# Softmax attention on paired 64-row tiles: fp32r stacks, three score banks, values in two parts of 256 queries, outputs normalised on GpSimd

## The reference

```python
qkv = x @ qkv_w.T + qkv_b                       # x: [4, 1024, 256]
qkv = jnp.transpose(qkv.reshape(B, S, 3, 16, 16), (2, 0, 3, 1, 4))
q, k, v = (qkv[0], qkv[1], qkv[2])              # [4, 16 heads, 1024, 16]
scores = jnp.einsum('bhqd,bhkd->bhqk', q, k) / sqrt(16)
attn = jax.nn.softmax(scores, axis=-1)
out = jnp.einsum('bhqk,bhkd->bhqd', attn, v)
out = jnp.transpose(out, (0, 2, 1, 3)).reshape(B, S, E)
return out @ out_w.T + out_b
```

## Time and profile before

| | |
|---|---|
| median of 3 runs | 2549.8 us |
| profiled execution, own time | 2556.4 us |
| its span, first to last instruction | 2554.6 us |
| mean granted TensorE clock | 0.942 |
| busy: PE, DVE, ACT, GpSimd | 2278.0, 1613.1, 1345.3, 644.6 us |
| stages (us of the span) | projection 0 to 119.5, attention to 986.8, feed-forward to 1221, the rest to 2554.6 |
| maxima on DVE (L509) | 512 of 1220 ns |
| exponentials on ACT (L667) | 1024 of 598 ns |
| scores, maxima, values on PE (L574, L567, L582) | 1024, 1024, 2048 instructions |

### The profile page before, as it was taken

How to read it: one execution, slowest core, us unless ns; L and a number is a source line. 1 busy time by engine, 2 the same in 40 slices (tenths; PEclk the granted TensorE clock), 3 DMA queues, 4 the chain that set the end, 5 groups by cost and what they waited for, 6 DMA issues and landing times. The chain is left out here.

```text
span 2554.6 us, 41316 instructions
## 1 busy us (share of the span) xinstructions
PE 2278.0 (89%) x14644; PEld 1462.9 (57%) x14644; DVE 1613.1 (63%) x2762; ACT 1345.3 (53%) x2589; POOL 644.6 (25%) x407
## 2 busy tenths in 40 slices
PE   7779999999999994787579999999999999588886
PEld 4412222222222222676568888888888888477775
DVE  5588788877878852677435445454545534568876
ACT  5517777777777773454254344444434444354551
POOL 3400000000000000355423325233332523234432
PEclk9859999999999997898789999999999999799998
DMA  6831211211121002111330213121220311200100
GB/s 193 241 77 54 55 40 39 73 41 39 39 73 41 6 7 88 34 50 50 120 100 26 93 38 105 52 67 52 67 93 28 115 51 59 66 17 26 33 17 25
DMA packets 129296, 159.02 MB, mean 62 GB/s; under 512 B 29896, under 2 KB 111952, under 8 KB 125008
## 3 DMA queue, kind: packets, MB, share of 16 engines
q1 hardware_dynamic: 129104, 156.47, 20.6%
HBM read 117.76 MB, written 38.27 MB: 61 GB/s over the span
## 5 line engine op out<-in xcount | busy, mean ns | idle before, releaser
L509 DVE TENSOR_REDUCE att_sb_mx<-att_ps_psM 128x1 f32<-128x1024 f32 x512 | 608.4, 1220 | 151.0 <-PE att_ps_psM L567 143.7
L667 ACT ACTIVATE att_sb_pt<-att_ps_psS 128x512 f32<-128x512 f32 x1024 | 586.2, 598 | 209.4 <-PE att_ps_psS L574 193.7
L574 PE MATMUL att_ps_psS<-att_sb_q,att_sb_k 99*128 99x512 bf16 x1024 | 392.7, 386 | 30.5 <-ACT att_sb_pt L667 12.0
L574 PEld LDWEIGHTS att_ps_psS<-att_sb_q,att_sb_k 99*128 99x128 bf16 x1024 | 96.9, 96 | 458.4 <-ACT att_sb_pt L667 406.4
L567 PE MATMUL att_ps_psM<-att_sb_k,att_sb_q 96*128 96x512 bf16 x1024 | 321.2, 396 | 28.5 <-DVE att_sb_ident_b L503 23.2
L582 PE MATMUL att_ps_psO<-att_sb_pt,att_sb_v 128*32 128x512 f32 x2048 | 273.9, 607 | 1.0 <-ACT att_sb_pt L667 1.0
L163 POOL MEMSET ffn_sb_half<- 128x4 f32 x1 | 0.1, 107 | 853.5 <-POOLq L184 853.5
L1922 ACT ACTIVATE gla_sb_sg<-gla_ps_psP 128x512 f32<-128x512 f32 x64 | 38.2, 598 | 277.1 <-PE gla_ps_psP L1683 277.1
L2256 POOL TENSOR_TENSOR gla_sb_dm<-gla_sb_dm,gla_sb_masked 128x1024 f32<-128x1024 f32 x64 | 158.5, 2498 | 90.5 <-DMA gla_sb_dm<-decay_rows 90.2
L1939 ACT ACTIVATE gla_sb_dm<-gla_sb_dm,gla_sb_neg_g 128x128 f32<-128x128 f32 x512 | 156.4, 391 | 10.1 <-POOL gla_sb_dm L2256 10.1
L567 PEld LDWEIGHTS att_ps_psM<-att_sb_k,att_sb_q 96*128 96x128 bf16 x1024 | 99.1, 100 | 107.7 <-DVE att_sb_mx L509 31.3
(11 more groups left out here) (256 smaller groups left out, 4917.0 us busy)
## 6 DMA issues: line engine op xcount, KB each, us to landing
gla_sb_dm<-decay_rows SPq DMA_DIRECT2D x32, 1024.0 KB, 5.8
gla_sb_eg<-decay_exp SPq DMA_DIRECT2D x64, 256.0 KB, 6.7
qk_parts<-qkv_sb_part SPq DMA_DIRECT2D x64, 192.0 KB, 3.1
values<-qkv_sb_va SPq DMA_DIRECT2D x32, 256.0 KB, 3.5
att_sb_v<-values SPq DMA_DIRECT2D x32, 256.0 KB, 3.7
att_sb_q<-qk_parts SPq DMA_DIRECT2D x32, 192.0 KB, 3.1
att_sb_k<-qk_parts SPq DMA_DIRECT2D x32, 192.0 KB, 3.0
qkv_sb_xin<-in_x SPq DMA_DIRECT2D x8, 512.0 KB, 5.1
```

The costliest lines, as they stand in the source:

```text
L509: nc.vector.tensor_reduce(mx[:, t // NT, t % NT:t % NT + 1], psM[:, t % 2, :], AX.X, ALU.max).then_inc(maxima_free, 1)
L574: pe.matmul(psS[:, j % 2, :], k[0:ROWS, g, j, s * P:(s + 1) * P], q[0:ROWS, g, qh, j, :], start=True, stop=True).then_inc(scores_done, 1)
L667: nc.scalar.activation(pt[:, s % 2, j, :], psS[:, j % 2, :], ACT.Exp).then_inc(exp_done, 1)
```

## The change

- **Stacks.** Queries and keys are split into two fp32r parts instead of three bf16 ones. A stack has three blocks (`Q_PART`, `K_PART`), 48 rows, and 2 rows for the maximum, against minus ones on the keys' side. The heads of a pair stand two and two: even heads in SBUF rows 0 to 63, odd heads in rows 64 to 127. A score matmul uses one half of the rows, the maxima matmul written beside it the other.
- **Score banks.** `psS` has three banks instead of two; the bank for the outputs' transposes (`psX`) goes, and the maxima are turned in the ring itself, at step 5 instead of 2.
- **Values** go in two parts of 256 queries, behind the third and the fourth score of a step.
- **Maxima** run half a unit less ahead (`AHEAD = 8` tiles beyond the next unit), 24 tiles in the prologue. GpSimd splits them (two operations instead of DVE's four).
- **Outputs.** They are not transposed any more. Four DMAs lay the sums out on 128 partitions (`den`), DVE takes the reciprocal, it goes to DRAM and back as a broadcast (`rb`), GpSimd multiplies 128x512, and SP stores the outputs with features on rows (`att_t`). All in `sums` and `out` on SP and `normalize` on GpSimd.
- **SP's order** per unit is `sums` of the unit before, in first halves the load of a later pair, the maxima rows of the next unit (the fourth waits for GpSimd's multiply), the outputs' store.
- **Projection.** Weights and tokens are split into two fp32r parts and multiplied in three passes; ACT writes one part, DVE the other.
- **Feed-forward.** `turn_projected` and `copy_projected` go; two DMAs a tile load the attended tokens as they are needed.

The core of the diff:

```diff
-Q_PART = (0, 1, 2, 0, 0, 1)
-K_PART = (0, 1, 0, 1, 2, 0)
+Q_PART = (0, 0, 1)
+K_PART = (0, 1, 0)
 STACK = len(Q_PART) * AD
-ROWS = STACK + 3
+ROWS = STACK + 2
+HALF_PE = P // 2
...
+        PASSES = ((whi, xhi), (whi, xlo), (wlo, xhi))
...
-        psS = m.ps("psS", [P, 2, ST])
+        psS = m.ps("psS", [P, 3, ST])
         psO = m.ps("psO", [P, ST])
-        psX = m.ps("psX", [P, NT, P])
...
+            def rows(b, g, qh, finished=None):
+                u = unit(b, g, qh)
                 sp.wait_ge(rows_ready, u + 1)
+                for a in range(2):
+                    for r in range(2):
+                        p = HALF_PE * r + STACK + a
+                        if a and r and finished is not None:
+                            sp.wait_ge(on_ready, finished + 1)
+                        sp.dma_start(q[p:p + 1, g, qh, :, :].bitcast(F32).rearrange("p j t -> p (j t)"),
+                                     mrow[TILES * a + 8 * r:TILES * a + 8 * r + 8, :].bitcast(F32)).then_inc(rows_in, 16)
+
+            def sums(u, w):
+                sp.wait_ge(osb_ready, u + 1)
+                for j in range(HG):
+                    sp.dma_start(den[VW * j:VW * (j + 1), w, :], osb[VW * j:VW * j + 1, w, :]).then_inc(den_in, 16)
+                sp.wait_ge(rden_ready, u + 1)
+                sp.dma_start(dens[w].rearrange("(p c) -> p c", p=P), rden[:, w, :]).then_inc(rden_out, 16)
+                sp.wait_ge(rden_out, 16 * (u + 1))
+                for j in range(HG):
+                    sp.dma_start(rb[VW * j:VW * (j + 1), w, :],
+                                 dens[w, j * ST:(j + 1) * ST].rearrange("(a c) -> a c", a=1).to_broadcast([VW, ST])
+                                 ).then_inc(rb_in, 16)
...
+                    if not start:
+                        sums(unit(pb, pg, pq), pq)
+                    nb, ng = (b, NG - 1) if g == 0 else (b + 1, g - 1)
+                    if qh == 0 and not (isinstance(nb, int) and nb >= BATCH):
+                        load_first(nb, ng, minus_set[ng] if start else None)
+                        load_second(nb, ng)
+                    if not (last and qh == 1):
+                        rows(*unit_after(b, g, qh), None if start else unit(pb, pg, pq))
...
+            def scores(b, g, qh, s, i, turning):
+                u, pos = unit(b, g, qh), place(s, i, turning)
+                r, j = ORDER[i] % 2, ORDER[i] // 2
+                rs = slice(HALF_PE * r, HALF_PE * r + ROWS)
+                e = HG * (KT * u + s) + i
+                if turning and s == TURN_AT and i == 2:
+                    pe.wait_ge(rows_ready, u + 2)
+                else:
+                    wait_past(pe, ring_taken, e - 1 if turning and s == TURN_AT and i < 2 else e - 2)
+                pe.matmul(psS[:, ring_slot(pos), :], k[rs, g, j, s * P:(s + 1) * P], q[rs, g, qh, j, :],
+                          start=True, stop=True).then_inc(ring_done, 1)
...
+                for j in range(HG):
+                    mm = pe.matmul(psO[VW * j:VW * (j + 1), cols], v[:, g, s, VW * j:VW * (j + 1)],
+                                   pt[:, s % 2, j, cols], start=(s == 0 and part == 0), stop=(s == KT - 1),
+                                   tile_position=(0, VW * j), skip_group_check=True)
...
+                        for i in range(HG):
+                            scores(b, g, qh, s, i, not final)
+                            t = AHEAD + 2 * s + i // 2
+                            if t < TILES:
+                                if not final:
+                                    maxima_half(*nxt, t, i % 2)
+                            elif not last:
+                                maxima_half(*nxt2, t - TILES, i % 2)
+                            if i >= 2:
                                 if s:
-                                    values(g, u, s - 1)
+                                    values(b, g, qh, s - 1, i - 2)
...
+            def normalize(u, w):
+                pool.wait_ge(rb_in, 64 * (u + 1))
+                if not (isinstance(u, int) and u < 2):
+                    pool.wait_ge(on_out, 16 * (u - 1))
+                nc.gpsimd.tensor_tensor(on[:, w, :], osb[:, w, :], rb[:, w, :], ALU.mult).then_inc(on_ready, 1)
```

More of the change, by code:

```diff
@@ L293, in body @@
[L293 to L300 removed]
+                    stats_of_x(i + 1, 1 - u)
@@ L302, in _ @@
+                for mt in range(2):
+                    low_part(i, u, mt)
+                if not last:
+                    normalize_x(i + 1, 1 - u)
+                for mt in range(2, 4):
+                    low_part(i, u, mt)
+                if not last:
+                    take_turned(i + 1, 1 - u)
+                for pair in range(2):
+                    take_values(i, u, pair)
             over_supertiles(dve, body)
@@ L480, in _ @@
+                load_second(0, g)
             rows(0, 0, 0)
             def body(b, g, last):
-                rows(b, g, 1)
-                nb, ng = (b, NG - 1) if g == 0 else (b + 1, g - 1)
-                if not (isinstance(nb, int) and nb >= BATCH):
-                    sp.wait_ge(pv_done, CREDIT + 2 * KT * (NG * b + g))
-                    load(nb, ng)
-                if not last:
-                    rows(*after(b, g), 0)
-                out(b, g, 0)
-                out(b, g, 1)
+                for qh in range(QH):
+                    start = isinstance(b, int) and b == 0 and g == 0 and qh == 0
+                    pb, pg, pq = (b, g, 0) if qh else ((b, g - 1, 1) if g else (b - 1, NG - 1, 1))
+                    if not start:
[7 more added lines that the diff above has]
+                    else:
+                        sp.wait_ge(on_ready, unit(pb, pg, pq) + 1)
+                    if not start:
+                        out(pb, pg, pq)
@@ L539, in _, with reciprocal @@
-            for qh in range(QH):
-                maxima(0, 0, qh, range(TILES))
-                split_maxima(0, 0, qh)
+                    if t == 0 and not (isinstance(u, int) and u < 2):
+                        dve.wait_ge(split, 2 * (u - 1))
+                    nc.vector.tensor_reduce(mx[:, qh, 8 * r + c:8 * r + c + 1], psM[:, t % 2, :], AX.X,
+                                            ALU.max).then_inc(maxima_taken, 1)
+            def reciprocal(u, w):
+                dve.wait_ge(den_in, 64 * (u + 1))
+                nc.vector.reciprocal(rden[:, w, :], den[:, w, :]).then_inc(rden_ready, 1)
@@ L670, in body @@
-                        if s == 3 and not (last and qh == 1):
-                            copy_rows(u + 1)
+                        if s == TURN_AT and not final:
+                            copy_rows(u + 1, (HG * s + 1) % 3)
+                        for i in range(HG):
+                            exponentials(u, s, i, not final)
+                            if s == 0 and i == 2 and not start:
+                                copy_outputs(u - 1, 1 - qh)
             over_pairs(act, body)
-            copy_outputs(2 * NBG - 1)
+            copy_outputs(2 * NBG - 1, 1)
@@ L925, in turn_x @@
                 pe.wait_ge(xn_ready, NT * (i + 1))
-                pe.wait_ge(aT_ready, KD * NST if isinstance(i, int) and i == NST - 1 else KD * (i + 2))
+                if not first(i, 1):
+                    pe.wait_ge(xlo_ready, KD * i)
                 for k in range(KD):
@@ L998, in _ @@
         def _(act):
-            def copy_projected(i):
-                for k in range(KD):
-                    act.wait_ge(a_turned, KD * i + k + 1)
-                    if k == 0 and not first(i, 1):
-                        act.wait_ge(a_done, i)
-                    nc.scalar.copy(aT[:, k, :], psT[:, k, :]).then_inc(aT_ready, 1)
             def take_turned(i, u):
```

529 lines of the change are left out of this document (258 added, 271 removed).

## The result

| | before | changed kernel |
|---|---|---|
| median of the runs | 2551.05 us (4 runs) | 2647.68 us (4 runs, 2632.07 to 2659.84) |
| ratio | | 1.037, 95% interval 1.031 to 1.043 |
| profiled execution, its span | 2556.4, 2554.6 us | 2653.5, 2651.7 us |
| granted TensorE clock over the span | 0.942 | 0.872 |

The forecast was 2498 us, with a range of 2440 to 2590. The runs of the changed kernel lie 1% apart, with mean granted clocks from 0.872 to 0.886, those of the kernel before 0.2%.

A forecast was written before the change was run, and what follows sets the result against it. Attention's step was taken as ACT's 2.33 us plus a 0.72 hole from PE's values block. Attention -50 (units 763 against 805, prologue, tail), projection 0, feed-forward -2: -52 on the median 2549.8 gives 2498 us, range 2440 to 2590.

The forecast's parts named there:

- The clock term: Attention's second halves: PE's clock can fall in a wait of about 4 us, adding 1.3 us to each.
- the clock stays at 1.2 GHz: Rival: the new attention loop runs at half clock, PE's step about 4.0 us, a unit 33, total 2790; chance 0.05.
- The step's sum: Attention's key step, all engines laid out in written order: mostly 2.46 to 2.64 us, 21.7 us a unit.
- A wait for a maxima bank comes on top: Attention's key step: long slots use 0.64 of 0.68 us slack; a maxima bank wait adds to that, not sized separately.
- PE's own sum: PE's work in a key step: score and maxima pairs 0.94, values 0.86, switches 0.48, together 2.28 us.
- The price of the switches: PE's tiling switches around values: 0.10 us going in, 0.14 coming out, 0.48 a step for two rounds.
- switches are dear: Rival: tiling switches on PE cost more, units 22.7 and 24.1 (2521 us) or 23.9 and 25.0 (2545); chance 0.22.
- The SP chain: Attention's first halves: SP's sums, load and row DMAs in sequence take 25.2 us, 26.3 with waits, against 21.7 of work.
- SP is cheap: Rival: 0.46 us a DMA issue, first halves 23.7 us, no clock fall, attention gains 101, total 2447; chance 0.20.
- take turns: Rival: scores and maxima of two row halves don't overlap; step 3.33 us, attention 919, total 2600; chance 0.08.
- ACT isn't unbound: Rival: a wait for a maxima bank or the row transpose brings back the 3.05 us step, total 2545; chance 0.05.
- Projection, prologue, tail, feed-forward: Terms outside the attention units: projection 0 (between -7 and +8), prologue -17, tail +9, feed-forward -2 us.

The follow-up runs named there:

- e4: The kernel before, with the next pair's rows issued late so that PE pauses in 13 pairs: 2651.2 us, 1.038 of before.
- e6: The changed kernel with 20 matmuls on 48 rows in each of the 12 pauses: 2649.2 us, 1.037 of the kernel before.
- e11: The changed kernel with 16 matmuls on all 128 rows ahead of the second step of 12 second halves behind a pause: 2626.5 us, 1.029 of before.
- e9: As e2, with the load's issues interleaved into SP's waits and the hardware loop over the batch written out: 2412.4 us, 0.946 of the kernel before.
- e2: As e1, with the two values parts behind the second and fourth scores of a step: 2523.4 us, 0.985 of the kernel before.
- e1: The changed kernel with the load of a pair spread over both halves: 2499.8 us, 0.980 of the kernel before.
- e5: The changed kernel with 20 matmuls on all 128 rows in each of the 12 pauses: 2570.3 us, 1.006 of the kernel before.

## Why the prediction was wrong

**The clock term failed.** "I add 1.3 us to each second half" took the one case that the trace of before had, 3.4 us at 0.51 behind a pause of 2.73 us, and carried it to another loop. 16 us were forecast, 112 came. The case was read rightly for its own loop: e4 gave that loop 13 longer pauses and each cost it 6.8 to 10.2 us at 0.50. The new loop's scores and maxima work on 64-row tiles, and with them the clock stays down far longer: 6.8 to 71.7 us. e6 and e11 point to the rows as the reason; a run that changed the rows of the loop itself, and nothing else, was not made. The rival "the clock stays at 1.2 GHz" named the right resource and even the reason ("streams through part of the array") and got 0.05. It came true for 352 of 905 us, with a step of 4.32 us for its 4.0. What it had wrong is "stays": at full clock the steady loop holds it, 92.6 us at a stretch here and 635.7 in e9. In the steady loop it takes pause and loop together; the last unit, without maxima, lost the clock with no pause at all.

The Trainium skill (TensorE: Matmul & The Clock Gate, Part 1: The HAM clock gate) says that sustained matmuls release the clock within some microseconds. e4 agrees: its clock was back 3.4 to 6.5 us after PE went on. The 71.7 us at 0.50 with PE busy 71.44 of them disagree, and the measurement decides.

**The step's sum was 43 us short.** Forecast 2.46 to 2.64 us a step and 692 us for all units without pauses and clock, measured 2.84 and 734.9. "A wait for a maxima bank comes on top" is the term that was mis-sized: it comes in every step (PE's next maxima half starts 0.28 us behind its scores, 203.00 to 203.28), since the half that waits for the bank stands ahead of both values parts, and the reduction that frees the bank starts 0.57 us behind a half that stands between them. PE's own sum was short by 0.10 for each pair behind values: 2.28 + 0.20 = 2.48, where e2 shows 2.46. The price of the switches, 0.10 in and 0.14 out, was right (0.09 and 0.14), so "switches are dear" falls.

**The SP chain was right in kind, and its sum partly by luck.** Twelve waits of about 4 us were forecast, which made 55 us of longer halves (26.3 - 21.7 each); eleven of 5.2 us on the mean came, 56.9 us. Most of these first halves took 27.7 to 29.5 us where 26.3 were forecast, so the chain was longer than its sum, and the longer step took up most of the difference. The load was 11.9 us by 18 issues, forecast 10.7; in the hardware loop it is 12.8 (442.0 to 454.84). "SP is cheap" falls, and so does its condition: in e2 the clock fell at nine of 13 pauses of 1.3 to 2.2 us. e1 shows the chain to be the cause of the pauses.

**The row tiles overlap**, as read from the earlier trace rows; "take turns" falls. ACT isn't unbound, though: at full clock it still stands 0.67 us a step (0.72 before), and with the pauses and the slow stretches its idle time for scores rose from 193.7 to 278.3 us.

**Projection, prologue, tail, feed-forward** were right within 7 us each. The two misses in the units (43 and 96), 2 of the pauses and 2.2 of the jump make the 143 us between 763 and 905.6.

That e1 came out at 2499.8, where 2498 had been forecast, is chance: it has no pauses (the forecast had 55 us of them), the longer step (43 more) and 63 us at 0.50.

## What to carry over

Before a pause of PE is priced, look at what comes behind it: a loop on partial rows of the array ran for up to 72 us at half clock after a pause that a loop on 96 to 99 rows got over in 7 to 10. So the first thing to do with such a loop is to keep its DMAs' issues out of the chain that feeds it, and where a pause can't be avoided, 14 to 20 matmuls on all rows in or behind it paid for themselves here (77 us in e5, 21 in e11). Where a block on PE stands between two halves of a double-buffered tile, follow the bank round once: its period is the step's floor, and moving the block by one slot may take it away (2.84 to 2.46 us here).
